# Off-diagonal score maxima as pairs of 51-row products in the two row halves of the array, in a causal attention kernel

## What is computed

```python
xn = _layernorm(x, axis=-1)
q = (x @ q_w + q_b).reshape(Bx, Tx, NH, HD).transpose(0, 2, 1, 3)     # NH = HD = 16
...
att = jnp.einsum('bhqd,bhkd->bhqk', q, k) * (1.0 / np.sqrt(HD))
att = att + build_alibi_bias(NH, Tx)[None]                            # head slope * (key - query)
att = jnp.where(causal[None, None], att, -jnp.inf)
att = jax.nn.softmax(att, axis=-1)
y = jnp.einsum('bhqk,bhkd->bhqd', att, v)
...
return y @ o_w + o_b
```

## Time and profile before

| | |
|---|---|
| median of 3 runs | 2735.36 us (2729.39 to 2735.55) |
| the profiled execution, its own time | 2729.97 us |
| its span, first to last instruction | 2727.9 us |
| PE / DVE / ACT / POOL busy, share of the span | 95% / 85% / 76% / 50% |
| `attend` within the span | from about 870 us to the end |

### The profile page before, as it was taken

How to read it: one execution, slowest core, us unless ns; L and a number is a source line. 1 busy time by engine, 2 the same in 40 slices (tenths; PEclk the granted TensorE clock), 3 DMA queues, 4 the chain that set the end, 5 groups by cost and what they waited for, 6 DMA issues and landing times.

```text
span 2727.9 us, 57513 instructions
## 1 busy us (share of the span) xinstructions
PE 2598.3 (95%) x21670; PEld 1637.9 (60%) x21670; DVE 2321.1 (85%) x4175; ACT 2059.8 (76%) x3887; POOL 1373.4 (50%) x1768
## 2 busy tenths in 40 slices
PE   6779999999997999999999999999999999999998
PEld 4569989999996444545445454454544545455454
DVE  3468888888886998999989998899998999999993
ACT  2248878877884687888887887788887887887886
POOL 2235555555653365464654645546464464654644
PEclk9889999999998899999999999999999999999999
DMA  2015575545555646556474564655546556474540
GB/s 73 1 44 171 179 189 186 173 164 177 176 178 165 106 74 123 80 99 106 73 127 75 104 105 68 122 82 98 100 79 122 82 97 102 77 127 77 103 89 17
DMA packets 315172, 299.58 MB, mean 110 GB/s; under 512 B 97174, under 2 KB 265516, under 8 KB 314668
## 3 DMA queue, kind: packets, MB, share of 16 engines
q1 hardware_dynamic: 313344, 295.55, 50.9%
q10 hardware_dynamic: 1552, 0.36, 0.1%
HBM read 175.27 MB, written 120.06 MB: 108 GB/s over the span
## 4 chain that ended last, share of the span: by engine, by line
PE 54%; ACT 6%; DMA 5%; issue 1%; SPq 0%; DVE 0%; POOL 0%; POOLq 0%; ACTq 0%
PE t_y L1570 19%; PE t_r L1554 16%; PE t_a L1505 12%; ACT t_prob L1599 6%; DMA scr_m<-t_mrows 4%; PE t_a L1538 4%; PE t_r L1516 3%; DMA t_q<-scr_m 1%; DMA t_k<-t_blockb 0%; DVE t_mxc L1647 0%; ACT t_mrows L1616 0%; SPq L1411 0%; ACT t_near L1608 0%; SPq L1417 0%; POOL t_prob L1744 0%
## 5 line engine op out<-in xcount | busy, mean ns | idle before, releaser
L1599 ACT ACTIVATE t_prob<-t_r 128x512 f32<-128x512 f32 (+1 forms) x2432 | 1261.4, 599 | 289.5 <-PE t_r L1554 285.4
L1647 DVE TENSOR_REDUCE t_mxc<-t_a 128x1 f32<-128x512 f32 (+3 forms) x1920 | 1129.3, 643 | 105.4 <-PE t_a L1505 102.7
L1554 PE MATMUL t_r<-t_q,t_k 109*128 109x128 bf16 (+4 forms) x4608 | 831.7, 275 | 31.1 <-DMA t_q<-scr_m 20.9
L1505 PE MATMUL t_a<-t_k,t_q 99*128 99x512 bf16 (+3 forms) x2560 | 650.1, 320 | 1.5 <-DVE t_mxc L1647 1.0
L1750 POOL TENSOR_SCALAR_AFFINE_SELECT t_near<-t_near 128x512 f32<-128x512 f32 x512 | 332.7, 650 | 532.3 <-ACT t_near L1608 532.1
L1570 PE MATMUL t_y<-t_prob,t_v 128*32 128x512 f32 (+3 forms) x6144 | 588.0, 496 | 0.0
L1554 PEld LDWEIGHTS t_r<-t_q,t_k 102*128 102x128 bf16 (+1 forms) x4608 | 373.6, 98 | 342.9 <-ACT t_prob L1599 133.1
L1744 POOL TENSOR_SCALAR_AFFINE_SELECT t_prob<-t_prob 128x512 f32<-128x512 f32 x512 | 322.5, 637 | 276.9 <-ACT t_prob L1599 276.9
L1608 ACT COPY t_near<-t_r 128x512 f32<-128x512 f32 x512 | 307.5, 602 | 82.6 <-PE t_r L1516 65.6
L1505 PEld LDWEIGHTS t_a<-t_k,t_q 99*128 99x128 bf16 x2560 | 210.8, 98 | 228.5 <-DVE t_mxc L1647 155.0
L1570 PEld LDWEIGHTS t_y<-t_prob,t_v 128*32 128x32 f32 x6144 | 157.7, 109 | 257.3 <-issue 182.4
(11 more groups left out here) (199 smaller groups left out, 4129.2 us busy)
## 6 DMA issues: line engine op xcount, KB each, us to landing
t_q<-scr_q SPq DMA_DIRECT2D x384, 128.0 KB, 4.0
t_k<-scr_k SPq DMA_DIRECT2D x384, 128.0 KB, 6.6
scr_q<-j_part SPq DMA_DIRECT2D x96, 256.0 KB, 3.4
scr_k<-j_part SPq DMA_DIRECT2D x96, 256.0 KB, 2.5
scr_v<-j_v SPq DMA_DIRECT2D x32, 544.0 KB, 5.0
t_v<-scr_v SPq DMA_DIRECT2D x64, 272.0 KB, 8.1
p_x<-in_x SPq DMA_DIRECT2D x32, 512.0 KB, 4.3
scr_res<-j_x SPq DMA_DIRECT2D x32, 512.0 KB, 3.8
```

The source lines that it names most:

```text
L1505: mm = pe.matmul(abank[n % A_BANKS][:, x * w:(x + 1) * w], q_op[t % NG][0:KA, h0 + x, i * P:(i + 1) * P], k_op[t % NG][0:KA, h0 + x, k0:k0 ...
L1554: mm = pe.matmul(ring[n % RING_BANKS][:, s * w + lo:s * w + hi], k_op[g][0:deep, h0 + s, j * P:(j + 1) * P], q_op[g][0:deep, h0 + s, q0 + ...
L1599: nc.scalar.activation(prob[:, q % SLOTS, h0:h0 + m, 0:w], ring[n % RING_BANKS][:, 0:m * w].rearrange("p (h n) -> p h n", h=m), ACT.Exp).t ...
L1647: V.tensor_reduce(mxc[:, t % 2, k0 // 512, h0:h0 + m, i], abank[n % A_BANKS][:, 0:m * w].rearrange("p (h n) -> p h n", h=m), AX.X, ALU.max ...
```

## The change

**Maxima in halves.** The operand rows are laid out anew: a head of the first pair has its main 51 rows (3 for positions, three slots of 16) at partitions 0 to 50 and the other 48 at 51 to 98; a head of the second pair has its main rows at 64 to 114 and the others at 0 to 47, with zero rows between. `largest` now multiplies the main rows only, for two heads at a time, one in each half of the rows of the array, into the two banks of a slot 1024 columns wide. There are 15 units per group instead of 30, still with 40 matmuls and 14,336 columns. DVE reduces 1024 (or 768) columns in one instruction. PSUM holds two such slots (four banks) instead of three single banks, and the ring has three banks instead of four. `diag`, `exp` and `weigh` multiply as before (99 to 125 rows deep).

**Planner.** A `max` unit is charged a pair of matmuls at the price of one, plus 10 ns; no change of layout is charged for it. When nothing of `weigh` holds it, PE takes an `exp` or `diag` piece if ACT has under 1000 ns of work ahead, and a `max` if DVE has under 600. SP's list is sorted by due time: a group's loads go out in five portions 3 us apart, and the residual is read after the store of the sequence before.

**Others.** `join` is one reduction over the three sets of maxima. `scale` moves from DVE to POOL. Loads are 25 DMAs per group instead of 13 (two heads each), and the constants 12 instead of 5.

```diff
-    out = []
-    for i in range(1, QT):
-        for k0 in range(0, i * P, 512):
-            w = min(512, i * P - k0)
-            out += [(i, k0, w, h, per_bank(w)) for h in range(0, GH, per_bank(w))]
-    return out
+    units = [(i, 512, (h, h + 2)) for i in range(QT // 2, QT) for h in range(2)]
+    units += [(i, 384, (h, h + 2)) for i in (3, 7) for h in range(2)]
+    units += [(i, 256, (0, 2, 1, 3)) for i in (2, 6)]
+    units += [(1, 128, (0, 2, 1, 3))]
+    return sorted(units)
...
-A_BANKS, RING_BANKS, SLOTS = 3, 4, 6
+A_SLOTS, RING_BANKS, SLOTS = 2, 3, 6
...
+        behind = lambda n: max(0.0, pl.free[n] - now) + sum(e[3] for e in pl.todo[n])
+        dry = [k for n, bound, kinds in (("ACT", 1000, ("exp", "diag")), ("DVE", 600, ("max",))) if behind(n) < bound
+               for k in kinds]
         stay = [e for e in able if tiled and e[1] == "weigh" and e[0] < min(able)[0] + 0.1]
-        rank, kind, t, x = min(stay or able)
+        rank, kind, t, x = min(stay or [e for e in able if e[1] in dry] or able)
...
-            now += n * mm(w)
+            n = len(h) * (2 if w == P else 1)
+            now += n // 2 * max(mm(w), 112) + 10
...
-                for x in range(m):
-                    mm = pe.matmul(abank[n % A_BANKS][:, x * w:(x + 1) * w],
-                                   q_op[t % NG][0:KA, h0 + x, i * P:(i + 1) * P],
-                                   k_op[t % NG][0:KA, h0 + x, k0:k0 + w], start=True, stop=True)
+                for pair in range(len(heads) // 2):
+                    for i, k0 in blocks:
+                        for e in range(2):
+                            h = heads[2 * pair + e]
+                            mm = pe.matmul(abank[n % A_SLOTS][:, 512 * e + at:512 * e + at + w],
+                                           q_op[t % NG][MAIN[e]:MAIN[e] + NMAIN, h, i * P:(i + 1) * P],
+                                           k_op[t % NG][MAIN[e]:MAIN[e] + NMAIN, h, k0:k0 + w], start=True, stop=True)
+                        at += w
...
-                V.tensor_tensor(flat(mxj[:, :, :]), flat(mxd[:, z, :, :]), flat(mxc[:, z, 0, :, :]), ALU.min).then_inc(s_join, 1)
-                dve.wait_ge(s_join, 2 * t + 1)
-                V.tensor_tensor(flat(mx[:, z, :, :]), flat(mxj[:, :, :]), flat(mxc[:, z, 1, :, :]), ALU.min).then_inc(s_join, 1)
+                V.tensor_reduce(mx[:, z, :, :], mxc[:, z, :, :].rearrange("p h (c i) -> p h i c", i=QT),
+                                AX.X, ALU.min).then_inc(s_join, 1)
...
             if x == NQ - 1 and t + NG < GROUPS:
-                pl.order["SP"].append(("load", t, 0))
+                pl.issue += [(now + 3000 * z, "load", t, z) for z in range(LOAD_PIECES)]
```

More of the change, by code:

```diff
@@ L748, in first_group @@
             def first_group():
[L750 to L758, removed]
+                load_constants(sp, a, q0, k0, blockb, zeros, 0, s_qkv0)
                 sp.wait_ge(s_q_out, 96)
@@ L1140, in __init__ @@
         self.todo = {n: [] for n in ("ACT", "DVE", "POOL")}
-        self.row = {}
+        self.issue = []
     def when(self, *key):
@@ L1200, in maxima_in @@
         if all(("max", t, u) in pl.done for u in range(NU)) and all(("reduce", t, i) in pl.done for i in range(QT // 2)):
-            pl.give("DVE", max(pl.when("reduce", t, i) for i in range(QT // 2)), t - lead + 1, ("join", t, 0), 320,
+            ends = [pl.when("reduce", t, i) for i in range(QT // 2)] + [pl.when("max", t, u) for u in range(NU)]
+            pl.give("DVE", max(ends), t - lead + 1, ("join", t, 0), 220,
                     lambda end: pl.give("POOL", end, t - lead + 1, ("split", t, 0), 1250))
@@ L1212, in inverted @@
         def inverted(end):
-            pl.give("DVE", end, t + 0.5, ("scale", t, c), 370, scaled)
+            pl.give("POOL", end, t + 0.5, ("scale", t, c), 720, scaled)
         def swapped(end):
@@ L1221, in turned, with residual @@
         pl.give("ACT", end, t + 1.2, ("yhigh", t, c), 470, high)
-        if t % NG == 1 and c == 0:
-            pl.order["SP"] += [("residual", t // NG, 0)]
-            for x in range(OUTS):
-                for z in range(2):
-                    pl.give("POOL", end + 8000 + 3000 * (2 * x + z), t + 1.2 + 0.25 * x, ("shift", t // NG, 2 * x + z), 1300)
+        if t == 1 and c == 0:
+            residual(0, end)
+    def residual(b, end):
+        pl.issue.append((end, "residual", b, 0))
+        for n in range(2 * OUTS):
+            pl.give("POOL", end + 8000 + 3000 * n, NG * b + 2.2 + 0.12 * n, ("shift", b, n), 1300)
     def possible(kind, t, x):
         ready = 0.0
-        if kind in ("max", "rows", "out") and len(slot_freed) >= A_BANKS:
-            ready = pl.when(*slot_freed[-A_BANKS])
+        if kind in ("max", "rows", "out") and len(slot_freed) >= A_SLOTS:
+            ready = pl.when(*slot_freed[-A_SLOTS])
         if kind in ("exp", "diag") and len(ring_freed) >= RING_BANKS:
@@ L1238, in possible @@
                 ready = max(ready, pl.when("weighed", t - NG, NQ - 1) + 12000)
-        if kind == "diag" and NG * t + x // 2 >= 4:
+        if kind == "diag" and QT // 2 * t + x // 2 >= 2:
             n = QT // 2 * t + x // 2 - 2
@@ L1290, in plan @@
             slot_freed.append(("lift", t, 0))
-            pl.give("ACT", now + 165, rank, ("lift", t, 0), 200, lambda end, t=t: pl.order["SP"].append(("lift", t, 0)))
+            pl.give("ACT", now + 165, rank, ("lift", t, 0), 200, lambda end, t=t: pl.issue.append((end, "lift", t, 0)))
         elif kind == "exp":
@@ L1314, in plan, with last @@
             slot_freed.append(("sum", t, x))
-            last = lambda end, t=t: pl.order["SP"].append(("store", t, 0))
+            def last(end, t=t):
+                pl.issue.append((end, "store", t, 0))
+                if t + 1 < B:
+                    residual(t + 1, end + 6000)
             pl.give("DVE", now + 165, rank, ("sum", t, x), 616, last if x == OUTS - 1 else None, "slot")
     pl.settle(pl.FAR)
+    pl.order["SP"] = [e[1:] for e in sorted(pl.issue)]
     return pl.order
@@ L1378, in attend @@
         s_join = sem("t_max_joined")
+        s_ys = sem("t_y_scaled")
         s_mp = sem("t_split_step")
@@ L1391, in attend @@
         turn = {e: n for n, e in enumerate(in_ring)}
-        y_step = {e: n + 1 for n, e in enumerate(e for e in ORDER["DVE"] if e[0] in ("swap", "invert", "scale", "back"))}
+        y_step = {e: n + 1 for n, e in enumerate(e for e in ORDER["DVE"] if e[0] in ("swap", "invert", "back"))}
+        scaled = {(t, c): n + 1 for n, (t, c) in enumerate(e[1:] for e in ORDER["POOL"] if e[0] == "scale")}
         y_parts = {(t, c): n + 1 for n, (t, c) in enumerate(e[1:] for e in ORDER["ACT"] if e[0] == "yhigh")}
@@ L1551, in logits @@
                 for s in range(per_bank(w)):
-                    for deep, lo, hi in ((KM, 0, first), (KB, first, w)):
+                    for depth, lo, hi in ((KM, 0, first), (KB, first, w)):
                         if lo < hi:
+                            deep = depth[(h0 + s) // 2]
                             mm = pe.matmul(ring[n % RING_BANKS][:, s * w + lo:s * w + hi],
@@ L1712, in _ @@
                     invert(t, x)
-                elif what == "scale":
-                    scale(t, x)
                 elif what == "back":
@@ L1779, in _ @@
                     split(t)
+                elif what == "scale":
+                    scale(t, x)
                 elif what == "ylow":
```

203 lines of the change are left out of this document (108 added, 95 removed).

## The result

The changed kernel takes 2794.9 us (median of 4 runs, 2794.2 to 2795.5) against 2732.4: ratio 1.0234, 95% interval 1.0208 to 1.026. It is slower by about 62 us, outside the range of 2620 to 2785, and on the other side of the forecast.

A forecast was written before the change was run, and what follows sets the result against it. PE was taken as the bound: floor 26.6 plus waits 1.3 gives 27.9 us per group, 0.4 below 28.3, times 64 groups 25 us; from 2730 to 2705, as median 2710 us, range 2620 to 2785.

The forecast's parts named there:

- 24.6, 1.6 and 2.1: PE's time per group before the change, in us: column stream, layout changes, and waits with small exposures, of 28.3.
- PE's floor: PE in `attend` after the change: 26.2 - 2.8 + 3.2 = 26.6 us per group, 0.4 above before.
- The 0.093: PE's array: each change of layout loses 0.093 us, 1489 more changes costing 138 us.
- The 0.07: PE at each of 835 stretches of maxima: filling two halves with weights costs 0.07 us, 58 us together.
- Stream: Maxima on PE: halves side by side take 3.3 us per group instead of 6.1, saving 2.8.
- the changes: PE's added layout changes, with filling and late weights behind them: 207 us together, 3.2 per group.
- Waits: PE's waits for other engines fall from 2.1 to 1.3 us per group, bounds 0.8 and 2.1.
- Ring and slots: PSUM: three ring banks hold 1.67 us of ACT's work, four held 2.2; two slots hold about what three did.
- The start: SP's first loads: the first `lift` stands behind one set instead of two, counted as nothing.
- DVE: DVE's work drops from 25.9 to 23.1 us per group, by itself no gain as PE stays the bound.
- Rival C: PE and its followers: too few PSUM banks, waits 2.9, group 29.5 us, 2790 to 2830 us; chance 0.15.
- Its sign: What would show the too-few-banks rival: PE idle on ACT and DVE more than 2 us per group.

The follow-up runs named there:

- b_tile: Kernel before, same order, each matmul of maxima only 51 rows deep, one head at a time, the smaller products left out: 2921.2 us, ratio 1.0697.
- a_chst: Changed kernel, planner charging 110 ns per layout change, group 2's first loads ahead of the first lift: 2762.8 us, ratio 1.0119.
- a_fullp: Changed kernel with maxima as full-array products, planner charging their true price, group 2's first loads ahead of the first lift: 2768.3 us, ratio 1.0129.
- a_full: Changed kernel, same orders, slots and banks, but maxima multiplied in the full array, one head after another: 2826.0 us, ratio 1.0352.
- b_a4r3_dry: Kernel before with four single banks for maxima, three ring banks and the rule on dry engines: 2735.8 us, ratio 1.0008.
- a_start: Changed kernel with only SP's first loads ordered as before, groups 1 and 2 both ahead of the first lift: 2784.9 us, ratio 1.0202.
- b_ring3: Kernel before with three ring banks instead of four, order planned anew, the change's condition on diagonal blocks: 2788.7 us, ratio 1.0217.

## Why the prediction was wrong

Step by step, along the prediction's own parts. The figures per group are those of the table above, which for the kernel before agrees with the prediction's own 24.6, 1.6 and 2.1:

- **PE's floor, 26.6 us, was about 1 us too high.** The mechanism held: at every change the weights come late and about 0.1 us is lost. The 0.093 was right (0.10 to 0.11 with the first load). The 0.07 for filling two halves was too much: a pair takes 0.32 us, 0.103 over one stream, and 0.093 of that is the change itself. Stream fell by 3.0 (2.8 forecast) and the changes cost 2.4 more (3.2 forecast): 21.4 + 4.1 = 25.5, or some 0.2 more at the prediction's slightly slower pace. What the prediction should have worked out is the sum for one pair between full products: 0.434 before, 0.32 + 0.11 = 0.43 after. For 512 columns the gain is nil, for 384 (0.328 against 0.27 + 0.11) it is negative. Only pairs that touch another pair or a `weigh` gain. `b_tile` shows the price alone.
- **What the halves are worth.** With each order planned at its right prices, halves take 2762.8 us (`a_chst`) and full products 2768.3 (`a_fullp`). The two ran in different sets, and their ratios (1.0119 and 1.0129) have intervals that overlap: the gain is 3 to 5 us and not clear of noise. The 31 us of `a_full` came from an order made for cheap pairs.
- **Waits, 1.3 us per group: the step that failed.** I let them fall from 2.1 because a PE that is later than planned would find the other engines finished. They rose: the rest is 3.6 us per group instead of 2.3, and `a_full` shows it as high (3.5) with no halves at all. The runs show how it grows. A ring of three with four banks for maxima and the rule has 2.6 (`b_a4r3_dry`), the double slots with what goes with them 2.8 (`a_fullp`), right prices with halves 3.1 (`a_chst`), wrong prices 3.6. So the planner's wrong price, which I counted as a help, costs 0.5 us per group, and 22 us in all (`a_start` 2784.9 to `a_chst` 2762.8). How it does so was not shown. My reading is that a late PE isn't late evenly: it is late after each pair, ACT's ring runs out, and then PE's next products find no bank.
- **Ring and slots.** I priced the ring by ACT's slack of 5 us per group and never by PE's. `b_ring3` shows 59 us for one bank. With a fourth bank for maxima it is 24, and the `dry` rule brings that to about nothing (`b_a4r3_dry`). I had written that two double slots hold about what three banks did, only less finely. The double slots and what wasn't separated from them cost some 19 us in the even pace.
- **The start, for which I counted nothing.** The changed kernel is 21 us behind by 1000 us. 10 of them are shown by `a_start`; the cause of the others wasn't tested.
- **DVE** fell less than forecast, 1.9 us per group instead of 2.8: it works 1243.5 / 51.5 = 24.1 (23.1 forecast). A reduction of 1024 columns takes 490.2 / 413 = 1.19 us (1.15 forecast).

The runs can be set in a row, by medians: 2729.9 (before), +6 for four and three banks with the rule, +32 for the double slots, the longer first lists and what goes with them, -5 for the halves, +22 for the wrong prices, +10 for the first loads: 2795. By the ratios of each set, which take out that the kernel before drifted from 2729.1 to 2733.1, the steps are +2, +33, -3, +23 and +9. Such a row adds up whatever its steps are; it says where the loss lies in this order of steps, and confirms nothing by its sum.

Rival C had the sign, and 2795 lies in its range. That is partly luck: its floor of 26.6 was about 1 us too high, its waits of 2.9 were 0.7 below the table's 3.6, and it had nothing for the start. Its sign, PE idle for more than 2 us per group, isn't there in PE's idle time (40 us in 1500, 0.8 per group), only in the late starts. I gave it 0.15, where the lost bank alone should have been run through PE's waits. None of the kernels tried beats the kernel before.

## What to carry to other kernels

Before packing small products side by side, work out one packed unit with both neighbours: here two changes of layout cost as much as the stream of 512 columns that they save, so packing pays only for units that stand together. And price a buffer by who fills it as well as by who empties it: ACT, which empties the ring, has some 5 us of slack in 28, and yet one ring bank fewer cost 59 us, as PE in front of it is late whenever it finds no free bank. Look for such a loss in the starts of the bound engine, not in the sum of its waits. A list order that is made from prices should get each new price from a trace before it is judged: here the wrong one cost 22 us.

## What the runs showed of the hardware

Two 51-row bf16 products in the two row halves take some 0.01 us more than the stream of one and the loss at the change behind it (0.32 us for 512 columns, 0.27 for 384). A change of layout costs 0.10 to 0.11 us for 64-row tiles, near the 0.09 on the way into 32-column tiles, and it falls on both sides. It falls too when a 51-row product has nothing beside it (`b_tile`). The Trainium skill ("TensorEngine Tiling (Array Packing)", Key Properties) says that changing the tiling mode drains TensorE; this case's rows agree and put 0.1 us on it.
